# A graph network kernel: one-hots of nine tiles' sources by one operation, and a bucket's ranks copied in four pieces

## The reference

```python
x = _layernorm(x + relations(x, ...))          # relu(segment_sum(h2[src, rel_type] * norm, dst) + bias2)
x = _layernorm(x + attention(x, ...))          # elu(segment_sum(x[src] * a, dst)), a: softmax over the edges of a dst
x = _layernorm(x + propagation(x, ...))        # twice: x = segment_sum(w * x[dst], src), w from node degrees
x = _layernorm(x + filters(x, edge_attr, ...)) # gate from edge_attr, segment_sum(gate * x[dst] * ..., src)
```

## Time and profile before

| | us |
|---|---|
| median of 3 runs | 5937.79 |
| the three runs | 5930.09, 5937.79, 5943.86 |
| the profiled execution, its own time | 5942.21 |
| its span, first to last instruction | 5940.3 |
| busy: PE / DVE / POOL / ACT | 3808.1 / 4197.8 / 4132.7 / 2341.0 |

### The profile page before, as it was taken

One profiled execution on the slowest core, in us unless ns is written; L12 is line 12 of the kernel. 1 busy time (PEld: TensorE's weight loads), 2 busy tenths in 40 slices (PEclk: granted clock), 3 DMA queues, 4 the chain that ended last, 5 costly groups with the idle time before them and its releaser, 6 DMA issues.

```text
span 5940.3 us, 125925 instructions
## 1 busy us (share of the span) xinstructions
PE 3808.1 (64%) x48224; PEld 2970.5 (50%) x48225; DVE 4197.8 (71%) x9427; ACT 2341.0 (39%) x3778; POOL 4132.7 (70%) x3857
## 2 busy tenths in 40 slices
PE   8355555555555553477777777777776588767764
PEld 7355554333333332255555555555554477666664
DVE  5555555666666666277787777777876966689998
ACT  2000000000000000366666666666665567777774
POOL 3677777777777776777777777777777312377774
PEclk7555555555555555555656556556555599978886
DMA  4666322222222221254444444544444266688885
GB/s 166 200 198 205 102 60 57 63 56 56 56 55 55 57 56 39 47 91 95 94 92 90 96 93 93 91 94 93 94 93 87 64 181 186 181 210 208 208 208 124
DMA packets 1414692, 652.72 MB, mean 110 GB/s; under 512 B 1069539, under 2 KB 1283823, under 8 KB 1413953
## 3 DMA queue, kind: packets, MB, share of 16 engines
q1 hardware_dynamic: 1309185, 533.53, 37.6%
q0 software_dynamic: 104896, 110.96, 8.6%
HBM read 475.32 MB, written 168.79 MB: 108 GB/s over the span
## 4 chain that ended last, share of the span: by engine, by line
POOL 50%; issue 17%; DVE 12%; PE 8%; DMA 7%; ACT 3%; SPq 3%; DVEq 0%; POOLq 0%; ACTq 0%
POOL ring L912 26%; POOL by_src L923 23%; DVE meta_b L2580 4%; DMA meta_b<-blocks 3%; PE ps L1481 2%; PE ps L1376 2%; ACT meta_b L1656 1%; PE ps L1078 1%; DVE dst_i L2590 1%; DMA by_src<-meta_a,row_src 1%; DVE meta_b L2708 1%; DMA meta_a<-in_attrT 1%; DMA ring<-h_table,meta_b 1%; DVE ring L2714 1%; SPq L784 1%
## 5 line engine op out<-in xcount | busy, mean ns | idle before, releaser
L923 POOL DMA_INDIRECT by_src<-meta_a,row_src x1612 | 1740.1, 1079 | 519.0 <-issue 482.0
L912 POOL DMA_INDIRECT ring<-h_table,meta_b x1616 | 1682.6, 1041 | 533.2 <-issue 487.6
L1244 PE MATMUL ps<-ring,WX 128*128 128x48 bf16 x2188 | 416.1, 237 | 960.7 <-DVE row_src L2211 960.6
L1244 PEld LDWEIGHTS ps<-ring,WX 128*128 128x128 bf16 x2188 | 364.6, 167 | 982.3 <-DVE row_src L2211 982.2
L1520 ACT ACTIVATE until_sorted<-until_sorted,halfpi 128x1612 f32<-128x1612 f32 x1 | 1.6, 1637 | 1972.2 <-DVE until_sorted L1910 1972.2
L1282 PE MATMUL ps<-meta_a,w1T 40*48 40x256 f32 x806 | 406.5, 603 | 475.2 <-DMA meta_a<-in_attrT 314.2
L1596 ACT ACTIVATE rb<-rb,place_c 128x1152 int16<-128x1152 int16 x478 | 596.2, 1247 | 157.8 <-DMA rb<-dst_rows 156.6
L1376 PE MATMUL ps<-WX,meta_b 128*128 128x49 bf16 (+1 forms) x14742 | 621.2, 205 | 15.3 <-ACT meta_b L1606 11.5
L1376 PEld LDWEIGHTS ps<-WX,meta_b 128*128 128x128 bf16 x14742 | 595.2, 111 | 24.9 <-ACT meta_b L1606 12.3
L1606 ACT ACTIVATE meta_b<-rb,ones 128x1152 bf16<-128x1152 int16 x478 | 598.9, 1253 | 19.9 <-PE ps L1376 0.4
L2580 DVE TENSOR_TENSOR meta_b<-big,meta_a 128x1152 bf16<-128x1152 bf16 x546 | 540.6, 990 | 0.0
(11 more groups left out here) (338 smaller groups left out, 8481.1 us busy)
## 6 DMA issues: line engine op xcount, KB each, us to landing
rb<-src_rows SPq DMA_DIRECT2D x273, 288.0 KB
rb<-dst_rows SPq DMA_DIRECT2D x273, 288.0 KB
meta_b<-blocks SPq DMA_DIRECT2D x490, 144.0 KB, 2.5
by_src<-default SPq DMA_DIRECT2D x44, 1456.0 KB
meta_a<-by_src SPq DMA_DIRECT2D x273, 216.0 KB, 3.5
rb<-lo_rows SPq DMA_DIRECT2D x202, 256.0 KB
blocks<-at_table SPq DMA_DIRECT2D x229, 144.0 KB
meta_a<-in_attrT SPq DMA_DIRECT2D x402, 80.0 KB
```

Of the source, the lines that this page charges most:

```text
L912: pool.indirect_dma_start(ring[:, gg % RING, j, 0:width], None, table, bass.IndirectOffsetOnAxis(ap=index(g * GROUP + j), axis=0)) \
L923: pool.indirect_dma_start(by_src, bass.IndirectOffsetOnAxis(ap=row_src[:, t:t + 1], axis=0), rec[:, q % RECS, j, :], None).then_inc(s_sc[q ...
L1244: mm = pe.matmul(acc_of(FROM[T] + h, FEAT), hot_w[:, g % 2, h, :, j], rows, start=False, stop=False, skip_group_check=True)
```

## The change

It has two parts. The first makes `ohK_n` as `ohS_n` is made: one `tensor_tensor` for nine tiles, which compares `lo_k` (now bfloat16, 9 slots of 50 cells that follow each other) with `place_of`. The tile is innermost, so each tile's one-hot, which PE reads as the moving operand, now has a step of 18 bytes from column to column. The second splits the `copy_predicated` of a bucket's ranks into four, one for each scanned piece. Each is issued at the start of the next piece, ahead of its wait for PE, and `mark_cells` follows the fourth.

```diff
-        lo_k = at_table[:, 0:8 * PER_SRC].bitcast(F32).rearrange("p (s j) -> p s j", s=8)
-        ohK_n = dst_i[:, 0:SG * P].bitcast(BF16).rearrange("p (s j n) -> p s j n", s=2, j=SG)
+        lo_k = at_table[:, 0:SG * PER_SRC // 2].bitcast(BF16)
+        ohK_n = dst_i[:, 0:SG * P].bitcast(BF16).rearrange("p (s n j) -> p s n j", s=2, j=SG)
...
-                        mm = pe.matmul(bank(5, P, at=i * P), ohS_n[:, a % 3, :, u * TRIO + i], ohK_n[:, a % 2, u * TRIO + i, :],
+                        mm = pe.matmul(bank(5, P, at=i * P), ohS_n[:, a % 3, :, u * TRIO + i], ohK_n[:, a % 2, :, u * TRIO + i],
...
+            def take_ranks(c):
+
+                b, i = divmod(c, 4)
+                ts = slice(i * ICH, (i + 1) * ICH)
+                dve.wait_ge(s_scan2, c + 1)
+                link(dve.copy_predicated(scratch[:, ts], hit[:, b % 2, ts].bitcast(U16), count[:, ts]))
+                if i == 3 and b + 2 < N_BUCKETS:
+                    mark_cells(b + 2)
+
             def cell_piece(c):
                 b, i = divmod(c, 4)
+                if c >= 1:
+                    take_ranks(c - 1)
                 dve.wait_ge(s_step2, c + 1)
-                if i >= 1:
-                    dve.wait_ge(s_scan2, c)
                 t0 = i * ICH
                 dve.tensor_tensor_scan(count[:, t0:t0 + ICH], bank(5 + i % 2, ICH), zeros_b[:, 0:ICH],
                                        count[:, t0 - 1:t0] if i else 0.0,
                                        ALU.add, ALU.add).then_inc(s_scan2, 1)
-                if i == 3:
-                    dve.wait_ge(s_scan2, c + 1)
-                    link(dve.copy_predicated(scratch, hit[:, b % 2, :].bitcast(U16), count))
-                    if b + 2 < N_BUCKETS:
-                        mark_cells(b + 2)
...
+                take_ranks(PIECES - 1)
                 link(dve.tensor_scalar(scratch[:, end], scratch[:, end], keep, None, ALU.mult))
...
-                dve.tensor_copy(lo_k[:, d % 8, :], fields[:, :, R_LO - FEAT])
+                dve.tensor_copy(lo_k[:, d % SG * PER_SRC:(d % SG + 1) * PER_SRC], fields[:, :, R_LO - FEAT])
...
                     if a >= 2:
                         dve.wait_ge(s_blk, 3 * (a - 1))
-                    for d, j0, j1, at in pieces(a):
-                        for j in range(j0, j1):
-                            dve.tensor_scalar(ohK_n[:, a % 2, at + j - j0, :], iota_b[:, 0:P], lo_k[:, d % 8, j:j + 1], None,
-                                              ALU.is_equal)
+                    at = a * SG % (SG * PER_SRC)
+                    dve.tensor_tensor(ohK_n[:, a % 2, :, :], lo_k[:, at:at + SG][:, None, :].to_broadcast([P, P, SG]),
+                                      place_of, ALU.is_equal)
```

## The result

| | before | after |
|---|---|---|
| median of 12 runs, us | 5941.1 (5930.1 to 5949.3) | 5955.1 (5949.1 to 5960.6) |
| profiled execution: its time / span, us | 5942.2 / 5940.3 | 5960.6 / 5958.4 |
| last gather call L912 starts at | 2341.0 | 2293.7 |
| last scatter call L923 starts at | 4600.7 | 4609.0 |

The changed kernel takes 1.0023 of the time before (95% interval 1.0014 to 1.0032), 14 us more. 5897 was forecast; the time lies in the range, but it moved the other way. The two spans differ by 18 us, and the starts of the last calls divide that: the gather stage gained 47 us, the scatter stage lost 56 (from 2370.5 to 4600.7, now from 2323.2 to 4609.0), and what is behind it lost 10 (1339.6 to 1349.4).

What follows compares the result with a forecast made beforehand. POOL's gather and scatter calls were taken as the bound. Ranks -33, one-hots -14, PE +8, behind the scatter -2 gave -41 us against the profiled 5942.2, 4.4 above the median: 5897 forecast, range 5845 to 5985.

Steps and rivals of the forecast that it cites:

- The ranks: Gather stage: each whole copy holds one POOL call, 64 us in all; pieces and exposed masks cost 29; 33 us gained.
- Random placement: Gather stage: with POOL's calls at random, a piece holds one in 44% of cases for 0.27 us, 24 us in all.
- The one-hots' holds: Scatter stage: one wide `build_K` beside `build_S` changes which POOL calls are held; half of 29 us taken, 14 us gained.
- the two placements of the forecast: Scatter calls starting 0.19 (90 steps) or 0.71 us (133 steps) after `build_K` begins; each would lose 0.19 us less, 42 us.
- PE's stepped read: L1416 beside the scatter: 0.24 us a matmul instead of 0.11, covered by ACT's waits; 8 us lost for late records.
- Rival (2): Scatter stage: PE becomes the bound, records come 0.25 us late for each quad, 100 us lost, 6000 us; chance 0.10.
- Behind the scatter: The 136 us stretch after the scatter: 6.1 us a step becomes 5.5 to 6.7; 2 us gained, bounds 13 either way.
- rival (4): Gather and scatter calls fall between DVE's operations: 64 + 60 us gained, 5830 us; chance 0.07.

Runs made afterwards that it cites:

- k_tile: Kernel before with the nine comparisons as one operation writing the tile outermost, ranks copied as before, PE reading contiguously: 5967 us, 1.0035 of 5940.
- the single rounds: Three runs of the kernel before, each with one of a step's three L1416 rounds reading in 18-byte steps: 5942, 5949 and 5935 us against 5940.
- tile_outer: Changed kernel, but the one operation writes the tile outermost, so L1416 reads 128 contiguous columns: 0.9929 of the kernel before, which took 7153 us there.
- whole: The whole change run again on a slower chip: 7345 us against 7153 for the kernel before, 1.0272.
- ranks_only: Kernel before with only the ranks copied in four pieces, one-hots as before, on a slower chip: 7030 us against 7067, 0.9956.

## Why the prediction was wrong, step by step

**The ranks: -33 forecast, -47 found.** Right in mechanism and low in size. The last gather call starts 47 us earlier, and L912's sum fell by 49 (1682.6 to 1633.6). The 196 copies last 0.612, not 0.56. The holds can be counted in the two traces, as what a call that starts inside an operation lasts above the median. Before, 49 calls start in a copy of the ranks and are held for 62.8 us in all, where 64 was forecast. With the change 56 are held in the pieces, for 10.4 us, where 24 was forecast, and 24 calls in the masks, for 5.0, where 5 was. Random placement, "44% of cases for 0.27 us", priced the pieces too high. Alone, the ranks gained on each of three chips (0.9956, 0.9972, 0.9955).

**The one-hots' holds: -14 forecast, -16 found.** Right in size, in one execution each. L923's time above its median fell from 178 us (1740.1 - 1612 x 0.969) to 142 (1708.7 - 1612 x 0.972). Counted by step, the calls that start from 0.1 us before `build_K` to the end of `build_S` are held for 100 us before and for 84 with the change; the other 20 us fell elsewhere, mostly at the subtractions. It isn't the two placements of the forecast carried over: POOL waits 104 us more, which shifts every call behind a wait. The same count in `k_tile` gives 152, so a wider operation does cost where it stands differently against POOL. One step of the forecast was luck: it lets a call go through that starts 0.02 ahead of `build_S`, while its own row of 2562.73, 0.02 ahead, was held, like all 90 calls of before that start less than 0.02 ahead. In the changed kernel 52 of 54 such calls did go through. Why they do isn't known. The rows show both operations holding calls, L2585 here:

```profile
3138.75 0.81 DVE L2585 TENSOR_TENSOR meta_b<-big,meta_a 128x1152 bf16<-128x1152 bf16 x1
...
3138.96 1.43 POOL L923 DMA_INDIRECT by_src<-meta_a,row_src  x1 [0.30 <-issue]
```

The call starts 0.21 into it and lasts 0.46 longer than 0.97, which is until 0.13 before the operation's end, as in the earlier trace rows.

**PE's stepped read: +8 forecast, 104 us of waits found. This is the step that failed.** Its first half was right: L1416 needs 0.237 us a matmul instead of 0.106 (medians of the starts within a round), where 0.24 was forecast. The second half was "covered by the 1.05 us that ACT waits for each quad", and has two faults. (The forecast for the scatter stage was -14 + 8, 6 us gained, and 56 were lost; the ranks and the stretch behind the scatter account for the rest of the miss, 14 and 12 us with opposite signs.) The row says 422.6 us in 163 times, 2.6 us in 163 quads and nothing in 240; dividing by 403 made an even cover out of an uneven one. And the price was set as PE's own time, 0.8 us a quad, 320 us by the prediction's sum, while the single rounds show 1.3 us of slack for a us of L1416. 320 looked safe beside 422; 443 does not. What is shown by experiment is that the stepped read alone costs 2.8% on a slower chip, and that each of its rounds alone eats slack on the fast one. That all three together made the 104 us of waits where the change was measured follows from the rows and these sums, with `k_tile` speaking against DVE; the run that would show it fell on another chip. Rival (2), which priced just this at 100 us of late records, was right to 4 us in that term, with luck: it had each of 403 quads 0.25 us late, and it was 87 waits of 1.6 us in the mean. It gave 6000 where 5955 came out, since the gather stage gained more and POOL's calls took less. It got 0.10 because of the slack and because a busier PE "may get more" of the clock. But the mean clock in the stretch went from 0.58 to 0.56, and a stepped read doesn't profit: within a round the starts are 0.237 us apart where half of full speed was granted (1.2 GHz, 1332 pairs) and 0.236 where all was (2.4 GHz, 300 pairs). The contiguous read of before does: 0.107 (1293 pairs) and 0.064 (339 pairs). So the same rounds lose most where the clock is full.

The Trainium skill (Advanced Engine Details and Errata, Memory Cachelines) speaks against the change in the prediction. The trace agrees, and shows it now for the moving operand alone: 0.237 against 0.106 us for 128 columns.

**Behind the scatter: -2 forecast, +10 found**, inside the bounds of 13 each way. Two things pull. One is the pace. From the last scatter to the last L1618 it is 138 us for 70 rounds before, 1.97 a round; in `k_tile`, with one operation instead of nine and the old read, 124 us for 70 rounds, 1.77, which is the upper bound of 13 us gained; and with the change 149 us for 76 rounds, 1.96. With the stepped rounds the gain in pace is gone. The other is that 6 rounds more, two steps, were left when the scatter ended. The stages behind take 1201 to 1202 us in all three. The chain of the changed kernel goes through L781 and L784, issues of many small packets, to a load that ACT waits for:

```profile
4619.13 6.17 SPq L784
...
4625.45 3.99 DMA rb<-src_rows
4629.46 1.26 ACT rb L1596
...
4631.24 0.88 PE ps L1416 x3
```

How much of the pace is SP's wasn't tried.

**The sum.** -47 + 56 + 10 = +19, against 18 between the spans; forecast was -33 - 6 - 2 = -41. The time of rival (4), 5830, doesn't follow from its own terms: -64 - 60 with the +8 and -2 of the rest gives 5820. Nothing hangs on it. DVE's own time was rightly priced at nothing: it is busy for 185 us less in all (4197.8 to 4012.6), and none of that shows in the time.

**A version that beats both.** The ranks alone, in every run they had, all on slower chips. `tile_outer` is better still there (0.9929), while its one operation alone is a loss of 0.35% where POOL is the bound; so which of the two is best depends on the chip. On the chip of the first measurement the ranks' gain is 47 us by the trace of the whole change. Neither version was timed there.

## What to carry to other kernels

A layout that saves one engine operations has a reader on another engine; price the read there before the write here. A cover is to be read as times and lengths, not as a sum over all steps, and charged with what the added work takes from the slack (here 1.3 to 1 over three rounds, but 0.9 to 1 for the first), not with its own duration. When a layout must change, look for the form that keeps the reader's columns contiguous and lets the writer pay, and where the slower work must stay, look at what stands behind it in its engine's order.

## What the runs showed of the hardware

- A moving operand in steps of 18 bytes costs 0.237 us for 128 columns at 1.2 GHz and 0.236 at 2.4; contiguous it is 0.107 and 0.064.
- A gather or scatter call that starts inside the copy of the ranks is held until 0.02 us before that operation's recorded end in the median (49 calls), one that starts inside `build_S` until 0.14 before it (138 calls in the trace before).
- The same 1152 comparisons last 0.815 us with the table's number stepping innermost, and 1.348 with it broadcast innermost (step 0). The Trainium skill (VectorE: DVE Perf Modes, Mode 2×_1P), on the mode of two results a cycle, asks for 16-bit operands with a step of 1; the trace agrees in direction.
- The same program took 5940, 7065 and 7154 us on different chips, with mean granted clocks of 0.58 to 0.61; the changed kernel, traced on two of them, has the same 123894 instructions on both. The page of `whole` gives a quarter of its chain to something that it has no name for:

```profile
another core or an unknown queue 26%; PE 25%; DVE 18%; issue 15%; ACT 8%; DMA 4%; POOL 2%; SPq 1%; DVEq 0%; ACTq 0%; POOLq 0%
...
L1618 ACT ACTIVATE at_table<-ps 128x384 uint8<-128x384 f32 x817 | 400.3, 490 | 1548.7 <-remote 1390.9
```

In the changed kernel on the first chip L1618 never waited for anything "remote". The traces do tell what it waits for. All 237 of these waits stand ahead of the first round of a step, and in 236 of them the only signal that ACT waits for is that of L1416, the round before it on PE. That signal comes long after the round's recorded end. A first round of `whole`, and one of the changed kernel on the first chip:

```profile
4231.56 0.86 PE L1416 MATMUL ps<-dst_i,meta_b 128*128 128x128 bf16 x3
4235.55 0.49 ACT L1618 ACTIVATE at_table<-ps 128x384 uint8<-128x384 f32 x1 [4.35 <-remote]
```

```profile
3362.63 0.87 PE L1416 MATMUL ps<-dst_i,meta_b 128*128 128x128 bf16 x3
3363.53 0.49 ACT L1618 ACTIVATE at_table<-ps 128x384 uint8<-128x384 f32 x1 [1.26 <-PE ps L1416]
```

3.13 us lie between the end of the round and ACT's start in one, 0.03 in the other. Over the first rounds of `whole` the signal is 3.15 us late in the median, 1057 us in all; on the chips where before takes 5940 it is 0.014 us, in every version. The traces from the slower chips have 898 to 1095 us of it. In `ranks_only` there the scatter stage lasts some 700 us longer than in the kernel before on the first chip (2740.1 to 5670.9), so the late signals are enough for that; the gather stage lasts some 400 us longer than in the changed kernel, and its waits weren't followed. The late signal comes with the first rounds, hardly with the second and third. Whether PE's work there really ends later than recorded (the ends of matmuls are modelled in the profile) or only its signal comes late isn't known, nor is why. But it decides what a result is worth: the tile-outermost operation is a loss of 0.35% on one chip and part of a gain on another. The stepped read costs 2.8% where the signals are late, and a third of it at most 0.2% where they aren't; all of it, by the traces of the change, some 1%.
